# Attention ahead of a GRU: all four blocks of exponentials summed by GpSimd, and values weighed two blocks behind the scores

## The reference

```python
scale, shift = split(emb @ W_emb + b_emb)
xn = rms_norm(x, g_norm) * (1 + scale) + shift
q, k, v = heads(xn @ W_qkv)                  # 16 heads of 32 features
q, k = rms_norm(q, g_q), rms_norm(k, g_k)
attn = softmax(q @ k.T * 32 ** -0.5)
x = x + o + o @ W_out                        # o = attn @ v
x = x + gru(cond, x)                         # 512 steps in order, hidden size 512
x = x + causal_conv(x, w)                    # 4 taps a feature
x = x + causal_conv(x, w) + b
```

## Time and profile before

| | |
|---|---|
| median of the runs | 2203.03 us (2200.3 to 2204.99) |
| profiled execution | 2203.72 us |
| its span (first to last instruction) | 2201.9 us |
| mean granted TensorE clock | 0.992 of full |
| TensorE (PE) matmuls busy | 2127.0 us, 97% |
| VectorE (DVE) busy | 1387.8 us, 63% |
| ScalarE (ACT) busy | 1188.2 us, 54% |
| GpSimd (POOL) busy | 1126.0 us, 51% |

### The profile page before, as it was taken

The page is one execution under the profiler, slowest core; times in us unless marked ns, Lnnn a source line. Parts: engine busy times, 40 slices in busy tenths (PEclk is TensorE's granted clock), DMA queues, the critical chain, the costliest instruction groups (busy, mean ns, idle before and its releaser), DMA issues.

```text
span 2201.9 us, 184513 instructions
## 1 busy us (share of the span) xinstructions
PE 2127.0 (97%) x76736; PEld 1592.1 (72%) x76736; DVE 1387.8 (63%) x5092; ACT 1188.2 (54%) x5996; POOL 1126.0 (51%) x3891
## 2 busy tenths in 40 slices
PE   7999999999999999999999999999999999999997
PEld 2222222222389999999999999999999988888886
DVE  3344444344267777777777777777777777777775
ACT  3444454444255555555555555555555555555554
POOL 0143333323146556656556556555656666666665
PEclk9999999999999999999999999999999999999999
DMA  6000000001122221221222211222211100000001
GB/s 249 1 1 1 1 1 1 1 20 59 48 47 55 51 53 50 52 52 49 69 52 54 54 50 49 52 72 54 52 48 52 44 5 24 7 5 5 5 7 19
DMA packets 159135, 86.69 MB, mean 39 GB/s; under 512 B 126016, under 2 KB 154944, under 8 KB 158272
## 3 DMA queue, kind: packets, MB, share of 16 engines
q1 hardware_dynamic: 158896, 83.42, 14.1%
q10 hardware_dynamic: 144, 2.10, 0.3%
HBM read 26.37 MB, written 12.58 MB: 18 GB/s over the span
## 4 chain that ended last, share of the span: by engine, by line
PE 66%; DVE 4%; issue 1%; DMA 1%; POOL 0%; ACT 0%; POOLq 0%; SPq 0%; DVEq 0%
PE ps L1120 61%; PE ps L1148 6%; DVE arena L976 3%; DVE arena L993 1%; DMA arena<-arena 1%; POOL arena L1185 0%; ACT ps L1053 0%; DVE arena L982 0%; PE ps L1155 0%; DVE arena L988 0%; POOL arena L1189 0%; POOL arena L1191 0%; DVE arena L1025 0%; DVE seq L1006 0%; ACT arena L1084 0%
## 5 line engine op out<-in xcount | busy, mean ns | idle before, releaser
L1120 PE MATMUL ps<-whh,arena 128*4 128x128 f32 (+1 forms) x65536 | 1452.7, 246 | 34.6 <-DVE arena L993 27.1
L1120 PEld LDWEIGHTS ps<-whh,arena 128*4 128x4 f32 x65536 | 1311.1, 87 | 157.0 <-DVE arena L993 77.2
L976 DVE STREAM_TRANSPOSE arena<-ps 128x128 f32<-128x128 f32 x1024 | 434.3, 424 | 251.2 <-PE ps L1120 251.1
L1078 ACT ACTIVATE arena<-arena 128x8 f32<-128x8 f32 x1024 | 215.6, 211 | 649.7 <-DVE arena L976 627.9
L1185 POOL TENSOR_TENSOR arena<-tap,seq 128x32 f32<-128x32 f32 x1024 | 231.6, 258 | 256.1 <-DVE seq L1006 256.1
L384 DVE TENSOR_REDUCE top<-ps 128x2 f32<-128x1024 f32 x128 | 150.7, 1219 | 256.4 <-PE ps L631 256.3
L993 DVE TENSOR_TENSOR_SCAN arena<-arena 128x24 f32<-128x24 f32 x1024 | 214.1, 209 | 144.8 <-ACT arena L1089 144.8
L1053 ACT ACTIVATE ps<-arena 128x128 f32<-128x128 f32 x1026 | 269.7, 263 | 0.7 <-PE ps L1155 0.7
L1185 POOL TENSOR_TENSOR arena<-tap,arena 128x32 f32<-128x32 f32 x1024 | 231.2, 257 | 66.8 <-POOL arena L1195 66.8
L982 DVE STREAM_TRANSPOSE arena<-ps 128x64 f32<-128x64 f32 x1024 | 252.6, 247 | 10.8 <-PE ps L1120 1.1
L222 POOL TENSOR_TENSOR arena<-arena 128x2048 f32<-128x2048 f32 x16 | 72.8, 4549 | 353.1 <-ACT arena L295 353.1
(11 more groups left out here) (90 smaller groups left out, 1291.6 us busy)
## 6 DMA issues: line engine op xcount, KB each, us to landing
arena<-arena SPq DMA_DIRECT2D x240, 104.0 KB, 2.1
arena<-seq SPq DMA_DIRECT2D x128, 104.0 KB, 2.1
arena<-gi_d SPq DMA_DIRECT2D x256, 32.0 KB
gi_d<-arena SPq DMA_DIRECT2D x108, 52.0 KB, 1.6
seq<-in_x SPq DMA_DIRECT2D x4, 1024.0 KB, 17.6
arena<-arena SPq DMA_DIRECT2D x32, 128.0 KB, 2.1
whh<-in_w_hh SPq DMA_DIRECT2D x1, 3072.0 KB, 21.1
arena<-seq SPq DMA_DIRECT2D x24, 128.0 KB, 2.2
```

What stands on the lines that cost most here:

```text
L976: e.transpose(trn[:, h].rearrange("p q (i c s) -> p q c i s", c=2, s=2)[:, :, :, :, 0], bank[RN[h]][:, 0:P].rearrange("p (q c i) -> p q c ...
L1078: e.activation(r_d0[:, h].rearrange("p (i s) -> p i s", s=2)[:, :, 1], trn[:, h, 0, 0:2 * NH].rearrange("p (i s) -> p i s", s=2)[:, :, 0], ...
L1120: last = e.matmul(bank[dst[h]][32 * G:32 * G + B, 0:n], hv, wv[:, k, gates, G, 64 * h:64 * h + 64], start=False, stop=k2 == 1 and k == C - ...
```

## The change

GpSimd gets a third addition a step, `add_last`, which adds block 3 to `acc`; `sums` then multiplies ones with `acc` alone (one product instead of two) for every step but the last. `weigh` moves back by one block through the new `weigh_late`: phase A of step n holds `weigh(n - 1, 2)`, phase B holds `weigh(n - 1, 3)` and `sums(n - 1)`, and phases C and D hold `weigh(n, 0)` and `weigh(n, 1)`. With that `invert` moves behind `exponentials(n, 0)`, `heads_out` behind `maxima(n + 1, 1)`, `sums_x` ahead of `scores(n + 1, 1)`, and `squares_x` to the end of the step before.

```diff
+                def add_last(n):
+                    wait(g_acc, 3 * n + 2)
+                    wait(a_exp, 8 * n + 8)
+                    e.tensor_tensor(acc, acc, pT[:, (4 * n + 3) % NPT], ALU.add).then_inc(g_acc, 1)
...
                     add_third(n)
+                    if n + 1 < NS:
+                        add_last(n)
...
-                        m, k = divmod(i - NPT, 4)
-                        if k < 3:
-                            e.wait_ge(g_acc, 2 * m + (2 if k == 2 else 1))
-                        else:
-                            e.wait_ge(p_sum, m + 1)
+                        e.wait_ge(g_acc, 3 * m + max(k, 1))
...
-                    if n:
-                        invert(n - 1)
                     exponentials(n, 0)
...
                     if has_x(n):
-                        squares_x(n // 4 + 1)
+                        rms_x(n // 4 + 1)
                     if n + 2 < NS:
                         keep(0, n + 2)
-                    if has_x(n):
-                        rms_x(n // 4 + 1)
+                    if n:
+                        invert(n - 1)
                     exponentials(n, 1)
...
                     exponentials(n, 3)
+                    if has_x(n + 1):
+                        squares_x((n + 1) // 4 + 1)
...
+                    if n + 1 < NS:
+                        maxima(n + 1, 1)
+                    if n + 1 == NS:
+                        take(3)
                     if n:
                         heads_out(n - 1)
                     if n + 1 < NS:
-                        maxima(n + 1, 1)
...
                 def sums(n):
                     e.wait_ge(a_top, min(n + 2, NS))
-                    e.wait_ge(g_acc, 2 * n + 2)
-                    for last_block in range(2):
-                        src = pT[:, (4 * n + 3) % NPT] if last_block else acc
+                    if has_x(n + 1):
+                        e.wait_ge(a_rx, 2 * ((n + 1) // 4 + 1) + 1)
+                    e.wait_ge(g_acc, 3 * n + (3 if n + 1 < NS else 2))
+                    terms = [acc] if n + 1 < NS else [acc, pT[:, (4 * n + 3) % NPT]]
...
+                def weigh_late(n, j):
+
+                    if j >= 2:
+                        weigh(n, j - 2)
+                    elif n:
+                        weigh(n - 1, j + 2)
+                        if j:
+                            sums(n - 1)
...
                     if more:
                         scores(n + 1, 0)
-                    if n:
-                        weigh(n - 1, 3)
-                        sums(n - 1)
+                    weigh_late(n, 0)
                     shifted(n, 0)
...
+                    if has_x(n):
+                        sums_x(n // 4 + 1)
                     if more:
                         scores(n + 1, 1)
                     if ahead:
                         project(0, n + 2, range(3, 4))
-                    weigh(n, 0)
-                    if has_x(n):
-                        sums_x(n // 4 + 1)
+                    weigh_late(n, 1)
```

More of the change, by code:

```diff
@@ L224, in add_third @@
                 def add_third(n):
-                    wait(g_acc, 2 * n + 1)
+                    wait(g_acc, 3 * n + 1)
                     wait(a_exp, 8 * n + 6)
                     e.tensor_tensor(acc, acc, pT[:, (4 * n + 2) % NPT], ALU.add).then_inc(g_acc, 1)
+                def add_last(n):
+                    wait(g_acc, 3 * n + 2)
+                    wait(a_exp, 8 * n + 8)
+                    e.tensor_tensor(acc, acc, pT[:, (4 * n + 3) % NPT], ALU.add).then_inc(g_acc, 1)
                 e.memset(ident[:], 0.0).then_inc(g_const, 1)
@@ L501, in _ @@
                         add_out(n, 0)
-                for u in range(3, len(UNIT)):
+                for u in range(4, len(UNIT)):
                     take(u)
@@ L532, in sums_x @@
                     else:
-                        e.wait_ge(a_lsum, 4 * (b - 1) + 1)
+                        e.wait_ge(a_top, 4 * (b - 1) + 2)
                     for k in range(C):
@@ L578, in norm @@
                         e.wait_ge(a_rx, 1)
-                    if n >= 3 and s == 0 and has_x(n - 2):
-                        e.wait_ge(a_rx, 2 * ((n - 2) // 4 + 1) + 1)
                     e.wait_ge(a_sq[s], n + 1)
@@ L727, in sums @@
                     e.wait_ge(a_top, min(n + 2, NS))
-                    e.wait_ge(g_acc, 2 * n + 2)
-                    for last_block in range(2):
-                        src = pT[:, (4 * n + 3) % NPT] if last_block else acc
+                    if has_x(n + 1):
+                        e.wait_ge(a_rx, 2 * ((n + 1) // 4 + 1) + 1)
+                    e.wait_ge(g_acc, 3 * n + (3 if n + 1 < NS else 2))
+                    terms = [acc] if n + 1 < NS else [acc, pT[:, (4 * n + 3) % NPT]]
+                    for i, src in enumerate(terms):
                         for g in range(NG):
-                            last = e.matmul(bank[SS][32 * g:32 * g + 32], ones[:, 0:32], src[:, g], start=not last_block,
-                                            stop=bool(last_block))
+                            last = e.matmul(bank[SS][32 * g:32 * g + 32], ones[:, 0:32], src[:, g], start=i == 0,
+                                            stop=i + 1 == len(terms))
                     last.then_inc(p_sum, 1)
+                def weigh_late(n, j):
[5 more added lines that the diff above has]
+                            sums(n - 1)
                 e.wait_ge(d_const, 4)
@@ L791, in _ @@
                         norm(0, n + 2)
-                    weigh(n, 1)
+                    weigh_late(n, 2)
                     tile_x(n, 0, range(0, 1))
@@ L800, in _ @@
                     tile_x(n, 0, range(3, 4))
-                    weigh(n, 2)
+                    weigh_late(n, 3)
                     tile_x(n, 1, range(0, 1))
@@ L810, in _ @@
                     scores(n + 1, j)
-                    if j == 0:
-                        weigh(n - 1, 3)
-                        sums(n - 1)
-                    else:
-                        weigh(n, j - 1)
+                    weigh_late(n, j)
+                    if j:
                         gates(5 * j - 2, 5 * j)
@@ L831, in _ @@
                 gates(34, C * len(UNIT))
+                weigh(n, 2)
                 weigh(n, 3)
```

## The result

The changed kernel takes 2217.55 us, the median of four executions (2214.22 to 2220.96), against 2203.16 for the kernel before (four executions, 2200.3 to 2204.99). The ratio is 1.0068, with a 95% interval of 1.0055 to 1.008: slower, and 11.75 us above the predicted 2205.8, outside the range. The profiled execution took 2214.22 us, with a span of 2212.4.

The account below looks back on a forecast made before the run. Two limits nearly coincide: TensorE's work and the loop scores, maxima, shifted, exponentials. Terms -2.5 + 12.3 - 0.2 - 1.7 - 1.4 - 5.5 + 0.1 = +1.1 on 2203.72 give 2204.8; + 1.7 - 0.7 makes 2205.8, range 2199.5 to 2211.

Parts of the forecast that it names:

- Phase A -0.18: Attention, steps 1 to 14: one product between scores and shifted instead of three, 7.60 us for 7.78, -2.5 in all.
- phase B +0.88: Attention, steps 1 to 14: a fourth product between scores and shifted, where TensorE is the bound, +12.3 in all.
- GpSimd's waits: Attention, steps 6 and 10: the waits of sums for GpSimd go, -1.66 and -1.4; a third wait is in step 2.
- third rival: Attention: GpSimd becomes late, add_last misses sums, 1 to 2 us in three steps, 2208 to 2211; 8%.
- Waits for the maxima: Attention: TensorE's waits for VectorE grow from 2.1 by 14 times 0.35, to some 7 us.
- Step 2: Attention, phase A of step 2: 13.23 us with a clock fall and a GpSimd wait, 7.60 without them.
- half a fall: Clock within steps 1 to 15: one fall to 1.2 GHz costs 3.4 us; half of one taken, +1.7.
- -5.45: Attention, phase A of step 2: gain if clock fall and GpSimd wait go, beside the 0.18 counted in phase A.
- case of repeated falls: Second rival, attention: phase A's hole makes the clock fall again, 3.4 us each; two falls 17%, more 4%.
- +1.1: Whole kernel: sum of all terms, added to the profiled execution's 2203.72 us, if the clock never falls in steps 1 to 15.
- 1.7 for the clock: Attention: the changed kernel put at half a clock fall of 3.4 us, added to 2204.8.
- three rivals: Attention: TensorE's work alone counts (2182.9, 6%; milder 2200, 10%); repeated clock falls (17%, more 4%); GpSimd late (8%).

Follow-up runs that it names:

- e14: The changed kernel once more, nothing altered, one execution for a second trace: 2202.03 us.
- e1: The kernel before with 16 semaphore increments at the start of TensorE's list: 2213.01 us, ratio 1.0049.
- e2: The kernel before with 45 semaphore increments at the start of GpSimd's list: 2200.79 us, ratio 0.9994.
- e8: The kernel before with 100 semaphore increments at the start of GpSimd's list: 2203.09 us, ratio 1.0001.
- e15: The kernel before once more, nothing altered, one execution: 2206.05 us.
- e13: The changed kernel with 16 semaphore increments at the start of TensorE's list: 2208.27 us, ratio 1.0012 to the kernel before.
- e11: e10 with 23 semaphore increments at the start of GpSimd's list too: 2190.78 us, ratio 0.9943 to the kernel before.
- e10: e3 with 16 semaphore increments at the start of TensorE's list: 2189.66 us, ratio 0.9919 to the kernel before.
- e3: The changed kernel with products spread anew between phases A and B, and take(4) ahead of heads_out: 2190.07 us, ratio 0.9947 to the kernel before.
- e7: e3 with 112 semaphore increments at the start of TensorE's list: 2200.9 us, ratio 0.9986 to the kernel before.
- e5: The changed kernel with 240 semaphore increments on TensorE's list, 150 at its start and 90 ahead of the GRU: 2231.81 us, ratio 1.014 to the kernel before.
- e9: The kernel before with add_last and one product in sums, the order left as before: 2250.27 us, ratio 1.0194.

## Why the prediction was wrong

- **Phase A -0.18, phase B +0.88** a step: right. 7.60 and 8.64 (predicted 7.60 and 8.66), a middle step of 32.04 (190.31 to 158.28 is 32.03; predicted 32.05). The margin of 0.2 us in the earlier trace rows and the thin phase of the earlier trace rows told what TensorE's 97% in the earlier trace rows hid.
- **GpSimd's waits**: right. Step 6 lasts 32.04 instead of 33.01, -0.97 where -1.66 + 0.70 = -0.96 was expected; no `sums` waits, so the third rival fell. **Waits for the maxima**: 7.9 for a predicted 7.
- **Step 2**: the clock fell once; the forecast had put in half a fall. Mis-sized: 3.4 predicted for one, 1.63 measured, so that the half came out nearly right, by luck. In e14, where step 2 lasts 32.03 (121.22 to 153.25), it didn't fall there. The -5.45 holds against the profiled execution alone: step 2 takes 36.80 in it, and 34.64 or 34.65 in e1, e2, e8 and e15, which have the same attention. So 2.15 of it aren't the change's. Between executions without a fall in step 0, attention takes 600.43 before (e8) and 603.71 in the changed kernel (e14). The case of repeated falls didn't come.
- **Missed in the attention**: the 1.28 for `take(4)`. The prediction checked what stands behind `heads_out` in a middle step (`maxima(n + 1, 2)`, "which come a whole phase later") and not in step 15, where `take(4)` does. Attention came out at +3.96 in the profiled execution, for a predicted +1.1 and 1.7 for the clock.
- **The step that failed** is the sum itself: "+1.1 on the profiled execution's 2203.72 (span 2201.9 and 1.82 around it)". It takes the 1597 us behind the attention as a constant: no line there changes, and the sum has no term for them. They took +6.54: -3.90 in the first loop, +10.44 in the last. The cause of the latter is shown by doing it alone and undoing it: e1 gives the kernel before the same hole and 457.19 with sixteen idle instructions, e13 takes 5.7 of it from the changed kernel, and the rest goes with GpSimd's place (e11 against e10: 447.7 for 451.68). Why a place costs time stays open, and so does the -3.90, which lies within the spread of that loop. None of the three rivals was in that stage.

Of 11.75 us between forecast and median, 6.5 are the GRU in the profiled execution, 1.3 `take(4)`, -0.1 what is left of the attention; 3.3 lie between the profiled execution and the median of the four, and 0.7 is what I took off for the opposite reason.

## What to carry to other kernels

When an edit changes how many instructions stand ahead of a loop, the loop can cost more or less without a line of it changed: compare the traces stage by stage, and test with a few instructions that do nothing, in the shadow of the first wait, before the edit itself is judged. A product taken from TensorE was worth its time here only in a phase where TensorE was the bound; where the removed work was the cover of another engine's latency, move other work into its place (e3: phases of 7.78 and 7.24 instead of 7.60 and 8.64). If the result varies more than it should, a second and third trace of the same kernel tell the fixed part from the rest.

## What the runs showed of the hardware

- The last loop, some 520 instructions on TensorE, takes 456 to 458 us at the places 4 and 12 in blocks of 32 instructions (196 and 204 in blocks of 256) and 447 to 454 at the others. One weight load a pass is held up, for 0.21 or 0.165 us, always at the same number of the list. Nothing is fetched anew for it. The first row is of the DMA queues over the whole execution before, and shows the queue that moves 47 packets instead of 48 with TensorE's list 240 shorter; the second is of the window 1775:2180, in which no packet of that queue stands, neither before nor after, and one in all of another:

```profile
q8 instruction: 48, 0.79, 0.2%
...
q14 instruction: 1, 0.01, 0.0%
```

  The Trainium skill ("Runtime: NRT & Kernel Launch", Instruction fetch mechanics) says that instructions come in blocks of 256, and that a branch out of the loaded window stalls. Such a stall isn't what costs the time in this loop, since the rows show no fetch. Whether the border of a block matters in another way isn't shown: the two numbers at which a load is held up, 11732 and 11988, lie 256 apart, but no run has a slow place that would tell 256 from 32.
- A semaphore increment on TensorE isn't cheap in a row: 112 at the start put the first matmul at 18.06 (e7) and 150 at 23.88 (e5), 0.15 us for each one more. 90 of them ahead of the GRU are in a gap of 17.78, at most 0.20 each.
- TensorE went through waits of 0.44 us in every middle step at the full clock; a wait of 1.89 in step 9 of e9 was followed by windows at 0.75 and 0.82, the same wait in step 7 by none under 1.00. A step with the fall costs 2.9 more than before, one without it 1.2.
